# Graph network layer kernel: the first phase projects raw tiles with centred weights and finds each node's edge range by products on TensorE

## The chip, the cores and the metric

The kernel runs on one core of a Trainium2 chip. The metric is device time in microseconds (us) of one launch; smaller is better. Engines are TensorE (PE; PEld are its weight loads), VectorE (DVE), ScalarE (ACT), GpSimd (POOL) and SyncE (SP). A name with q (ACTq, SPq) is an engine's queue that issues a DMA.

## The reference

Two blocks of (graph layer, feed-forward layer) on 3125 nodes with 256 features and 50000 edges, sorted by target node. The change touches only what stands ahead of the first graph attention layer:

```python
def _layernorm(x, axis=-1, eps=1e-05):
    m = jnp.mean(x, axis=axis, keepdims=True)
    v = jnp.var(x, axis=axis, keepdims=True)
    return (x - m) / jnp.sqrt(v + eps)
...
        xh = (x @ W).reshape(N, H, D)
        a_src = jnp.einsum('nhd,hd->nh', xh, att_src)
        a_dst = jnp.einsum('nhd,hd->nh', xh, att_dst)
...
        e = jax.nn.leaky_relu(a_src[src] + a_dst[dst], NEG_SLOPE)
        m = jax.ops.segment_max(e, dst, num_segments=N)
...
    x = x + _L0_gnn_ref(_layernorm(x, axis=-1), edge_index, L0_gnn_W, ...)
```

The segment operations need, for each node, where its run of edges starts and ends in the sorted list.

## The kernel before

The program is a row of blocks; at the end of each all engines meet at a barrier, after their DMAs have landed. `first_phase` is the first block, `spread_phase` the second, `edge_phase` the third. Work inside a block is ordered by semaphores written out by hand; each engine runs its own list in order.

The nodes lie as NT = 25 tiles of P = 125 rows, in chunks of TB = 5 tiles. The edges lie as Q = 98 partitions with J = 4 pieces of EP = 128 edges each (`dstq`, `srcq`), and, turned by TensorE, as 128 partitions with ET = 392 columns (`dst_e`, `src_e`, `fwd_e`, `bwd_e`, `seat_e`).

`first_phase` does two things.

1. The projection. x is loaded whole into `res` (3 MB). After the whole has landed DVE takes each row's mean and variance (`norm_stats`), and ACT the root. Per chunk DVE writes the normed tiles `xn`, PE turns them (L359), ACT copies them out of the banks (L297), PE multiplies them with `w` (L366; 256 columns and 16 more for the attention sums, which DVE makes from W and att on L421 and L422), DVE adds the bias (L437). ACT's queue stores the result to the DRAM table `xh_tab`, SP's queue its last 8 columns to `adst_tab`.
2. The node bounds. For each node two counts: how many pieces of 128 edges begin ahead of it (15 tiles on DVE, L410, and 10 on ACT, L283, over the 392 first targets), then how many edges inside that piece lie ahead (L448). For the second count POOL gathers the piece of each node by 25 indirect DMAs (L331) from `dst_pad`, a copy of the targets in DRAM. The ends are the starts moved on by one node, which is done by a write to `start_tab` in DRAM and a read back (L260 to L263).

When `xh_tab` has landed POOL issues the 14 gathers of the first batch of edges (L176), still inside the block. `spread_phase` begins with 25 indirect scatters on POOL (L636), which need the bounds.

Of the kernel before, what the change touches and what calls it, by code (L numbers as in the profile page):

```python
# [19 lines left out]
I32 = mybir.dt.int32  # L20
U32 = mybir.dt.uint32
ALU = mybir.AluOpType
# [82 lines left out]
def setup(k):  # L105

    banks = k.ctx.enter_context(k.nc.psum_tensor("bank", [128, 8, 512], F32))
    k.ps = [banks[:, i, :] for i in range(8)]
# [23 lines left out]
    k.dst_pad = k.dram("dst_pad", [ET * EP])  # L132
    k.start_tab = k.dram("start_tab", [N + 1])
# [36 lines left out]
DVE_COUNTS = 15  # L170


# [7 lines left out]
def first_phase(k):  # L180
# [3 lines left out]
    ctx = ExitStack()  # L184
    with ctx:
        sb = lambda n, s, d=F32: k.sb(n, s, d, ctx)
        srcq_i, dstq_i = sb("srcq_i", [Q, J * EP], I32), sb("dstq_i", [Q, J * EP], I32)
# [3 lines left out]
        first_b = sb("first_b", [128, ET])  # L191
        last_b = sb("last_b", [128, ET])
        trash = sb("trash", [P, NT, ET])
        before = sb("before", [P, NT])
        tile = sb("tile", [P, NT])
        tiles_i = sb("tile_i", [128, NT], I32)
        tile_i = tiles_i[0:P, :]
        windows = sb("window", [128, NT, EP])
        window = windows[0:P, :, :]
        start, end, last = sb("start", [P, NT]), sb("end", [P, NT]), sb("last", [P, NT])  # L200
        has, t0 = sb("has", [P, NT]), sb("t0", [P, NT])
        total = sb("total", [1, 1])
        start_t, end_t = sb("start_t", [NT, P]), sb("end_t", [NT, P])
        starts_ready, starts_turned, ends_turned = k.sem("starts_ready"), k.sem("starts_turned"), k.sem("ends_turned")
# [4 lines left out]
        dummy = sb("no_edge", [1, RW])  # L209
        bias_in, bias_tail, dummies, dummies_out = k.sem("bias_in"), k.sem("bias_tail"), k.sem("dummies"), k.sem("dummies_out")  # L210
        xn = sb("xn", [P, TB, C])
        xt = sb("xt", [128, TB, 2, P])
        zeros = sb("zeros", [Q, J * EP // 2])
        zeroed, cleared, placed = k.sem("zeroed"), k.sem("cleared"), k.sem("placed")
        mark = sb("mark", [1, 1])
        w_in, att_in = k.sem("w_in"), k.sem("att_in")
        deviations, roots = k.sem("p_deviations"), k.sem("p_roots")
        w_ready = k.sem("w_ready")
        xn_made, xt_turned, xt_made = k.sem("p_xn_made"), k.sem("p_xt_turned"), k.sem("p_xt_made")
        projected, taken, out_done = k.sem("projected"), k.sem("p_taken"), k.sem("p_out_done")  # L220
        padded = k.sem("padded")
        edges_in = k.sem("edges_in")
        x_in = k.sem("x_in")
        banks_read = k.sem("banks_read")
        consts = k.sem("consts")
        edges_f = k.sem("edges_f")
        pad_out = k.sem("pad_out")
        turned = k.sem("turned")
        ends_b = k.sem("ends_b")
        tiles_found = k.sem("tiles_found")  # L230
        windows_in = k.gather_sem("windows_in")
        firsts_made, signs_summed, xh_done = k.sem("firsts_made"), k.sem("signs_summed"), k.sem("xh_done")
        half = sb("half", [P, NT])
        columns_made = k.sem("columns_made")
        starts_found = k.sem("starts_found")
        starts_out = k.sem("starts_out")
        ends_in = k.sem("ends_in")
        full = E // (J * EP)
        rest = E - full * J * EP
        even = full // 16 * 16  # L240

# [3 lines left out]
        def _(sp):  # L245
            sp.wait_ge(padded, 2)
            for a, t in ((k.a["dst"], dstq_i), (k.a["src"], srcq_i)):
                sp.dma_start(t[0:even, :], a[0:even * J * EP].rearrange("(q e) -> q e", e=J * EP)).then_inc(edges_in, 16)
            sp.wait_ge(edges_f, 1)
# [6 lines left out]
            for i in range(NT // TB):  # L256
                sp.wait_ge(taken, (i + 2) * TB)
                move(sp, adst_rows[:, i * TB:(i + 1) * TB, :], k.xh[:, i * TB:(i + 1) * TB, XW:RW], out_done)
# [12 lines left out]
        def _(act):  # L271
# [21 lines left out]
            for i in range(NT // TB):  # L293
# [4 lines left out]
                if i:  # L298
                    store(i - 1)
# [74 lines left out]
        def _(dve):  # L374
# [16 lines left out]
            for b, t in enumerate((k.dst_e, k.src_e, k.fwd_e, k.bwd_e, k.seat_e)):  # L391
# [3 lines left out]
                if b == 0:  # L395
                    dve.sem_inc(ends_b, 1)
# [2103 lines left out]
```

## Time and profile before

| | us |
|---|---|
| median of 3 runs | 1978.06 |
| lowest, highest | 1973.62, 1979.04 |
| the profiled execution, its time | 1977.53 |
| the profiled execution, its span | 1975.8 |

| engine | busy us of the span |
|---|---|
| PE | 1365.6 (69%) |
| PEld | 1134.1 (57%) |
| POOL | 1098.3 (56%) |
| DVE | 907.3 (46%) |
| ACT | 576.3 (29%) |

`first_phase` fills the first 100.6 us of the span. The profile gives every instruction's start and duration, the idle time of its engine just before it and what released it. A clock column shows what share of 2.4 GHz TensorE was granted: 1.00 is 2.4 GHz, 0.50 is 1.2 GHz.

### The profile page before, as it was taken

Reading aid. Unit: us, or ns where it says so; the run is one execution under the profiler, and the core shown is the slowest. Engines: PE = TensorE matmul, PEld = TensorE weight load, DVE = VectorE, ACT = ScalarE, POOL = GpSimd, SP = SyncE. Lnnn points to the kernel's source line nnn. Section 1 sums busy time; section 2 is a strip of 40 time slices with the busy share of each in tenths; the row PEclk is TensorE's granted clock in tenths of the full one; section 3 lists DMA queues with packets and bytes.
Section 4 is the critical chain, followed back from the end, with each engine's and each line's share of the span. In section 5 each row is a group of like instructions: output and inputs, shape, how many; then the busy total and the mean of one; then the engine's idle time right before and its main releaser. Section 6 shows DMA issues by size and latency. Waiting matters only on the chain. (4 is left out here: it accounts for less than half of the span.)

```text
span 1975.8 us, 23808 instructions
## 1 busy us (share of the span) xinstructions
PE 1365.6 (69%) x6688; PEld 1134.1 (57%) x6688; DVE 907.3 (46%) x1818; ACT 576.3 (29%) x1264; POOL 1098.3 (56%) x1086
## 2 busy tenths in 40 slices
PE   2435666656666266599999997656666666567998
PEld 2324544444454146599999997444445444346787
DVE  7425544444443667633333333644334333335953
ACT  2133433323333014133333332422222222222310
POOL 4477777777774600377222273077777777773520
PEclk7756878878878575699999999877878787978999
DMA  6484998888887601432111122743333333330002
GB/s 145 119 251 150 298 312 284 281 285 272 276 283 258 155 6 63 134 115 83 46 46 46 46 98 65 174 142 104 105 105 105 105 104 105 106 99 1 1 1 65
DMA packets 156809, 268.56 MB, mean 136 GB/s; under 512 B 26747, under 2 KB 119839, under 8 KB 155567
## 3 DMA queue, kind: packets, MB, share of 16 engines
q1 hardware_dynamic: 100252, 135.75, 22.1%
q0 software_dynamic: 46224, 123.97, 21.0%
q10 hardware_dynamic: 10213, 7.36, 1.5%
q8 instruction: 61, 1.00, 0.2%
q14 instruction: 59, 0.48, 0.1%
HBM read 169.82 MB, written 98.15 MB: 136 GB/s over the span
## 5 line engine op out<-in xcount | busy, mean ns | idle before, releaser
L1182 POOL DMA_INDIRECT sum_rows<-xn_tab,src_e x391 | 373.3, 955 | 174.5 <-issue 118.8
L1207 PE MATMUL bank<-sum_held,sum_hot 128*125 128x256 f32 x976 | 304.1, 474 | 195.3 <-ACT sum_held L1217 191.1
L798 POOL DMA_INDIRECT gat_rows<-xh_tab,src_e x363 | 343.4, 946 | 114.8 <-issue 107.8
L1207 PEld LDWEIGHTS bank<-sum_held,sum_hot 128*125 128x125 f32 x976 | 222.2, 236 | 273.5 <-issue 179.7
L871 PE MATMUL bank<-gat_rows,gat_same 128*128 128x264 f32 x784 | 263.7, 483 | 126.2 <-issue 126.2
L871 PEld LDWEIGHTS bank<-gat_rows,gat_same 128*128 128x128 f32 x784 | 176.6, 244 | 166.4 <-issue 132.6
L1217 ACT COPY sum_held<-sum_rows 128x1024 f32 x122 | 127.4, 1045 | 373.6 <-SPq L1173 334.1
L1894 PE MATMUL bank<-weights,e_xthigh 128*128 x896 | 220.3, 330 | 8.5 <-DVE e_xtlow L2049 5.4
L915 ACT COPY gat_outs<-bank 128x528 f32<-128x528 f32 x196 | 117.3, 598 | 281.8 <-PE bank L871 280.5
L2054 DVE TENSOR_TENSOR e_h<-e_gated,bank 128x342 f32<-128x342 f32 x112 | 57.1, 510 | 262.9 <-ACT e_gated L1987 262.9
L1239 DVE SCALAR_TENSOR_TENSOR res<-bank,prep_inv,res 125x256 f32 x122 | 58.9, 483 | 234.8 <-PE bank L1207 228.2
L1894 PEld LDWEIGHTS bank<-weights,e_xthigh 128*128 128x128 f32 x896 | 153.9, 192 | 17.9 <-issue 17.8
L1894 PE MATMUL bank<-weights,e_xtlow 128*128 x448 | 144.5, 323 | 0.0
L1915 PE MATMUL bank<-weights,e_hthigh 128*128 (+2 forms) x672 | 133.6, 294 | 0.3 <-DVE e_htlow L2059 0.3
L1987 ACT ACTIVATE e_gated<-bank 128x342 f32<-128x342 f32 x112 | 51.0, 455 | 239.2 <-PE bank L1894 239.2
L1773 POOL CAST weights<-staged 128x4264 fp32r<-128x4264 f32 x7 | 26.3, 3760 | 151.9 <-SPq L1832 142.8
L835 DVE TENSOR_TENSOR gat_rows<-gat_rows,bank 128x1792 f32<-128x1792 f32 x56 | 110.3, 2009 | 0.8 <-ACT bank L907 0.8
L1915 PEld LDWEIGHTS bank<-weights,e_hthigh 128*128 128x128 f32 (+2 forms) x672 | 102.5, 189 | 0.5 <-issue 0.5
L1915 PE MATMUL bank<-weights,e_htlow 128*128 x336 | 94.1, 280 | 0.0
L1894 PEld LDWEIGHTS bank<-weights,e_xtlow 128*128 128x128 f32 x448 | 85.9, 192 | 0.0
L819 DVE TENSOR_TENSOR gat_logit<-gat_rows,adst_e 128x112 f32<-128x112 f32 x28 | 7.8, 277 | 165.8 <-DMA gat_rows<-xh_tab,src_e 165.8
L1225 DVE TENSOR_TENSOR sum_hot<-bank,walk_local 128x2000 f32<-128x2000 f32 x31 | 69.0, 2225 | 2.2 <-DMA prep_bias<-in_L_gnn_b_dram 2.2
(508 smaller groups left out, 2416.8 us busy)
## 6 DMA issues: line engine op xcount, KB each, us to landing
parts<-gat_outs SPq DMA_DIRECT2D x27, 1904.0 KB, 8.0
staged<-w_tab SPq DMA_DIRECT2D x8, 2132.0 KB, 8.9
w_tab<-w_stage SPq DMA_DIRECT2D x16, 682.0 KB, 10.6
w_raw<-in_L_ffn_w_dram SPq DMA_DIRECT2D x16, 640.0 KB
gat_rows<-xh_tab,src_e POOLq DMA_INDIRECT x391, 4.7
sum_rows<-xn_tab,src_e POOLq DMA_INDIRECT x391, 2.8
w_tab<-w_stage SPq DMA_DIRECT2D x8, 768.0 KB, 10.6
weights<-y_tab SPq DMA_DIRECT2D x10, 600.0 KB
```

Of the source, the lines that this page charges most:

```text
L798: pool.indirect_dma_start(out=rows[b % R][:, t, :], out_offset=None, in_=k.xh_tab, in_offset=bass.IndirectOffsetOnAxis(ap=k.src_e[:, b * S ...
L835: v.tensor_tensor(f, f, weight[b % 2][:, t0 * H:t1 * H].rearrange("p (t h a) -> p t h a", h=H, a=1).to_broadcast([EP, SB // 2, H, D]), ALU ...
L871: m = nc.tensor.matmul(k.pairs[duo % DUOS][:, t % 2, 0:sums_w], same[b % 2][:, t, :], rows[b % R][:, t, 0:sums_w], start=True, stop=True)
L915: nc.scalar.copy(outs[b % 2][:, t:t + 2, 0:sums_w], k.pairs[duo % DUOS][:, :, 0:sums_w]).then_inc(taken, 1)
L1182: pool.indirect_dma_start(out=rows[:, at // IP % (RING * GPAIRS), at % IP, :], out_offset=None, in_=k.xn_tab, in_offset=bass.IndirectOffse ...
L1207: m = nc.tensor.matmul(k.ps[s][0:P, 0:C], hot[g % 2][:, s, c, :], held[:, s, c, :], start=(c == 0), stop=(c == IP - 1))
L1217: nc.scalar.copy(held_pair(n), pair).then_inc(staged, 1)
L1225: v.tensor_tensor(hot[g % 2][:, :, :, :], lane.rearrange("p (a b n) -> p a b n", a=1, b=1).to_broadcast([EP, IB, IP, P]), w.local[:, g * I ...
L1239: v.scalar_tensor_tensor(out=into, in0=k.ps[s][0:P, 0:C], scalar=prep.inv[:, bass.ds(node, 1)], in1=into, op0=ALU.mult, op1=ALU.add).then_ ...
L1894: last = nc.tensor.matmul(bank[:, 0:HH[a]], xt[s][px][:, c, :], part(slot, up_at(m, pw, c) + HB[a], 128, HH[a]), start=(n == 0), stop=(n = ...
L1915: m = nc.tensor.matmul(DOWN[s][:, 0:C], ht[a][ph][0:rows, b, :], part(slot, down_at(pw, 3 * a + b), rows, C), start=(a == 0 and n == 0), s ...
L2054: v.tensor_tensor(h[a][:, 0:HH[a]], gated[a][:, 0:HH[a]], GATE[a][:, 0:HH[a]], ALU.mult).then_inc(h_made, 1)
```

## The change

The x load is split into five chunk loads that start right behind the edge loads. The raw tile is turned and multiplied; the mean is taken out by centring the weights instead (each column of `w` less its mean, which PE sums with a matrix of ones and DVE subtracts), and 1/deviation is multiplied in when DVE takes the product. Statistics are made per chunk. The transposes of one tile stand ahead of the product of the tile before.

The bounds need no gathers. `passed[q, j, n]` is 1 where node n is beyond the first edge of piece j of partition q: four comparisons on POOL, each 98x3125. `rises` holds the differences between each piece of 128 targets and the piece before. The product of `passed` and `rises`, summed over all pieces (four matmuls per tile), is the piece that a node's run begins in; column 128 counts the pieces. The second count is then made from the bank, three tiles of each chunk on DVE and two on ACT. The ends come from two small products of `start` with a shifted identity and a corner matrix. The joins table is made for 8 partitions, later, in `spread_phase`. `dst_pad`, `start_tab`, the window gathers and the piece counts over 392 columns are gone.

```diff
         @block.sync
         def _(sp):
-            sp.wait_ge(padded, 2)
+            sp.wait_ge(padded, 3)
             for a, t in ((k.a["dst"], dstq_i), (k.a["src"], srcq_i)):
                 sp.dma_start(t[0:even, :], a[0:even * J * EP].rearrange("(q e) -> q e", e=J * EP)).then_inc(edges_in, 16)
-            sp.wait_ge(edges_f, 1)
-            sp.dma_start(k.dst_pad.rearrange("(q e) -> q e", q=Q), dstq[:, :]).then_inc(pad_out, 16)
-            move(sp, k.res[:, :, :], k.a["x"].rearrange("(t p) c -> p t c", p=P), x_in)
+            for c in range(CHUNKS):
+                move(sp, k.res[:, c * TB:(c + 1) * TB, :], x_rows[:, c * TB:(c + 1) * TB, :], x_in[c])
             sp.wait_ge(zeroed, 1)
...
+            for c in range(CHUNKS):
+                tiles = slice(c * TB, (c + 1) * TB)
+                sp.wait_ge(taken, (c + 1) * TB)
+                move(sp, xh_rows[:, tiles, :], k.xh[:, tiles, 0:XW], xh_done)
+            for c in range(CHUNKS):
+                tiles = slice(c * TB, (c + 1) * TB)
+                move(sp, adst_rows[:, tiles, :], k.xh[:, tiles, XW:RW], adst_out)
...
         @block.gpsimd
...
+            me(pool, nc.gpsimd.iota(node_row, pattern=[[1, N]], base=0, channel_multiplier=0, allow_small_or_imprecise_dtypes=True))
+            pool.wait_ge(firsts_made, 1)
+            for j in range(J):
+                nc.gpsimd.tensor_scalar(passed[:, j, :], node_row, first_dst[:, j:j + 1], None, ALU.is_gt).then_inc(passed_made, 1)
...
-            for t in range(NT):
-                pool.indirect_dma_start(out=windows[:, t, :], out_offset=None, in_=k.dst_pad.rearrange("(a b) -> a b", b=EP),
-                                        in_offset=bass.IndirectOffsetOnAxis(ap=tiles_i[:, t:t + 1], axis=0)).then_inc(windows_in, 16)
             pool.wait_ge(columns_made, 1)
-            pool.wait_ge(xh_done, 32 * (NT // TB))
+            pool.wait_ge(xh_done, 32 * CHUNKS)
             gather_batch(k, pool, 0)
...
         @block.tensor
...
+            pe.wait_ge(passed_made, J)
+            pe.wait_ge(rises_made, 1)
+            pe.wait_ge(taken, NT)
+            for t in range(NT):
+                c, s = t // TB, t % TB
+                if c:
+                    pe.wait_ge(tiles_kept, c)
+                    if s < BY_DVE:
+                        pe.wait_ge(counted, (c - 1) * BY_DVE + s + 1)
+                    else:
+                        pe.wait_ge(signed, (c - 1) * (TB - BY_DVE) + s - BY_DVE + 1)
+                for j in range(J):
+                    last_mm = nc.tensor.matmul(k.ps[XR + t % XP][0:P, 0:WIN], passed[:, j, t * P:(t + 1) * P], rises[:, j, :], start=(j == 0), stop=(j == J - 1))
+                last_mm.then_inc(windows, 1)
...
         @block.vector
...
+            for c in range(CHUNKS):
+                if c < CHUNKS - 1:
+                    spreads(c + 1)
+                take(c)
+            me(dve, v.tensor_copy(rises[:, 0, 0:EP], prev_i[:, :]))
...
+                dve.wait_ge(signed, (c + 1) * (TB - BY_DVE))
+                v.tensor_copy(tile[:, c * TB:(c + 1) * TB], k.banks[0:P, XR:8, EP]).then_inc(tiles_kept, 1)
```

The next excerpts are the engines' own lists. POOL, before, from the attention mask table to the first gathers (`window` is the piece gathered for each node of a tile):

```order
L324 AFFINE_SELECT sel<-sel 8x256
L326 AFFINE_SELECT sel<-sel 8x256
L331 DMA window<-dst_pad,tile_i 128x128 x25
L176 DMA gat_rows<-xh_tab,src_e 128x264 x14
L185 UNCONDITIONAL_BRANCH
```

POOL, of the change, from the row of lane numbers (`minus`) on:

```order
L288 IOTA minus 98x512
L289 MEMSET p_bias 125x16
L290 IOTA passed 98x3125
L293 TENSOR_SCALAR passed<-passed,first_dst 98x3125 x4
L294 MEMSET zeros 98x256
```

The 25 gathers are gone, and one long iota and four long comparisons stand where POOL had short setup work; the 14 gathers still end its list in the block. DVE, before, from the edges' landing to the first column table:

```order
L379 CAST dstq<-dstq_i 98x512
L381 CAST srcq<-srcq_i 98x512
L383 TENSOR_TENSOR same<-dstq 98x511
L384 MEMSET same 98x5
L385 COPY cont_q<-same 98x512
L386 TENSOR_SCALAR tile_dst<-dstq 98x4
L388 SCALAR_TENSOR_TENSOR seat<-same,minus 98x512
L389 SCALAR_TENSOR_TENSOR seat<-same,seat 98x512
L390 TENSOR_SCALAR same<-same 98x513
L393 COPY dst_e<-bank 128x4x98
```

DVE, of the change, the last of the same steps and what follows:

```order
L385 SCALAR_TENSOR_TENSOR seat<-same,seat 98x512
L386 TENSOR_SCALAR same<-same 98x513
L390 TENSOR_TENSOR prod<-w,att 128x512
L391 TENSOR_REDUCE w<-prod 128x2x8
L390 TENSOR_TENSOR prod<-w,att 128x512
L391 TENSOR_REDUCE w<-prod 128x2x8
L395 COPY dst_e<-bank 128x4x98
L395 CAST src_e<-bank 128x4x98
L395 COPY fwd_e<-bank 128x4x98
L395 COPY bwd_e<-bank 128x4x98
L395 COPY seat_e<-bank 128x4x98
L400 SCALAR_TENSOR_TENSOR w<-bank,w 128x272 x2
```

The nine edge steps keep their order; the work on the weights moves ahead of the five column copies, and the centring follows them. PE, of the change, the last tile of the second count's products and the block's end; nothing like it was there before, when L369 and L371 turned `start` and its shifted copy:

```order
L358 MATMUL bank<-rises,passed 125x129 [waits signed,tiles_kept]
L358 MATMUL bank<-rises,passed 125x129 x3
L362 MATMUL bank<-start,ident 125x25 [waits starts_made,corner_made]
L363 MATMUL bank<-start,corner 125x25
L183 UNCONDITIONAL_BRANCH
```

## Rows read from the trace of the kernel before

**Rows 1.** Timeline, the block's last 27 us: start, duration, engine, line [idle <-releaser].

```profile
73.39 0.36 ACTq L141 DMA_DIRECT2D xh_tab<-xh  x1
...
79.67 0.94 POOL L176 DMA_INDIRECT gat_rows<-xh_tab,src_e  x1 [21.29 <-DMA xh_tab<-xh]
...
85.42 0.18 DVE L455 COPY end<-bank 125x25 f32<-125x25 f32 x1 [4.39 <-PE bank L371]
...
87.33 0.18 DVE L466 TENSOR_SCALAR start_row<-t 125x25 int32<-125x25 f32 x1
...
95.92 0.94 POOL L176 DMA_INDIRECT gat_rows<-xh_tab,src_e  x1 [0.30 <-issue]
...
100.73 0.23 DVE L685 MEMSET tails<- 125x200 f32 x1 [13.22 <-PEq L185]
```

**Rows 2.** Timeline, the first instruction of the third block.

```profile
163.43 0.29 DVE L804 COPY bank<-lane 128x128 f32<-128x128 f32 x1 [7.28 <-PEq L604]
```

**Rows 3.** Timeline, DVE and POOL while both work on the first tables.

```profile
5.21 0.48 DVE L379 CAST dstq<-dstq_i 98x512 f32<-98x512 int32 x1 [4.06 <-DMA srcq_i<-in_src_dram]
5.48 0.46 POOL L324 TENSOR_SCALAR_AFFINE_SELECT sel<-sel 8x256 f32<-8x256 f32 x1
...
5.72 0.49 DVE L381 CAST srcq<-srcq_i 98x512 f32<-98x512 int32 x1
6.00 0.47 POOL L326 TENSOR_SCALAR_AFFINE_SELECT sel<-sel 8x256 f32<-8x256 f32 x1
...
6.14 0.88 DVE L383 TENSOR_TENSOR same<-dstq 98x511 f32<-98x511 f32 x1
```

**Rows 4.** Groups of POOL instructions: count | busy us, mean ns | idle before.

```profile
L1774 POOL TENSOR_TENSOR weights<-staged,weights 128x4264 fp32r<-128x4264 f32 x7 | 65.6, 9372 | 0.6
...
L1773 POOL CAST weights<-staged 128x4264 fp32r<-128x4264 f32 x7 | 26.3, 3760 | 151.9 <-SPq L1832 142.8 <-DMA staged<-w_tab 9.1
...
L1188 POOL CAST att_w_high<-att_w_comb 128x1024 fp32r<-128x1024 f32 x1 | 1.1, 1055 | 0.0
...
L308 POOL IOTA minus<- 98x512 f32 x1 | 0.6, 577 | 0.1
```

**Rows 5.** DMA issues in the first 102 us: count, size, us from issue to landing.

```profile
att<-in_L_gnn_att_dst_dram ACTq DMA_DIRECT2D x1, 128.0 KB, 9.7
```

**Rows 6.** Timeline: edge steps of DVE, a column copy, a product on the weights.

```profile
7.60 0.68 DVE L388 SCALAR_TENSOR_TENSOR seat<-same,minus 98x512 f32<-98x512 f32 x1
...
9.65 0.43 DVE L390 TENSOR_SCALAR same<-same 98x513 f32<-98x513 f32 x1
...
11.08 0.87 DVE L393 COPY dst_e<-bank 128x392 f32<-128x392 f32 x1 [1.01 <-PE bank L344]
...
26.66 0.69 DVE L421 TENSOR_TENSOR prod<-w,att 128x512 f32<-128x512 f32 x1
```

**Rows 7.** Timeline, DVE's row statistics; PE in the second chunk of the projection.

```profile
30.77 8.27 DVE L473 BATCH_NORM_STATS2 stats<-res 125x6 f32<-125x256 f32 x25 [1.25 <-DMA res<-in_x_dram]
...
48.62 1.60 PE L359 MATMUL bank<-ident,xn 125*128 125x125 f32 x10
...
54.65 0.59 PE L359 MATMUL bank<-ident,xn 125*128 125x125 f32 x4
```

**Rows 8.** Busy time by stretch: us, PE, PEld, DVE, ACT, POOL, PEclk, DMA, GB/s.

```profile
41.40:44.50 3.10, 3.06 (x13) 2.69 (x14) 2.81 (x9) 1.83 (x5) 2.49 (x3) 0.50 0.22 63
...
72.90:75.60 2.70, 0.00 (x0) 0.00 (x0) 2.68 (x18) 0.00 (x0) 0.00 (x0) 0.93 0.47 91
```

**Rows 9.** Timeline, first and last of twelve products of 128 columns on PE.

```profile
1910.39 0.39 PE L2265 MATMUL bank<-t_token,att_square 128*128 128x128 f32 x2
...
1912.84 0.39 PE L2267 MATMUL bank<-att_square,t_token 128*128 128x128 f32 x2
```

**Rows 10.** Timeline, one of ACT's signed counts over 392 columns.

```profile
17.10 0.60 ACT L283 ACTIVATE trash<-first_b,half 125x392 f32<-125x392 f32 x1
```

**Rows 11.** Groups of PE instructions: the products of 98 rows and 124 columns.

```profile
L994 PE MATMUL bank<-walk_pick,dstq 98*128 98x124 f32 x8 | 2.1, 440 | 0.0
```

More of the change, by code:

```diff
@@ L190, in first_phase @@
         seat, seat0, minus = sb("seat", [Q, J * EP]), sb("seat0", [Q, J * EP]), sb("minus", [Q, J * EP])
[L191 to L200, printed above, removed]
+        first_dst, rises = sb("first_dst", [Q, J]), sb("rises", [Q, J, WIN])
+        passed = sb("passed", [Q, J, N])
+        node_row = passed[:, J - 1, :]
+        trash = sb("trash", [P, TB, EP])
+        before, tile = sb("before", [P, NT]), sb("tile", [P, NT])
+        start, last, corner = sb("start", [P, NT + 1]), sb("last", [P, NT]), sb("corner", [P, P])
         has, t0 = sb("has", [P, NT]), sb("t0", [P, NT])
-        total = sb("total", [1, 1])
-        start_t, end_t = sb("start_t", [NT, P]), sb("end_t", [NT, P])
-        starts_ready, starts_turned, ends_turned = k.sem("starts_ready"), k.sem("starts_turned"), k.sem("ends_turned")
+        half = sb("half", [P, NT])
         w = sb("w", [128, 2, RW])
@@ L302, in _ @@
+            act.wait_ge(halves_made, 1)
+            for c in range(CHUNKS):
+                for t in range(c * TB + BY_DVE, (c + 1) * TB):
+                    act.wait_ge(windows, t + 1)
+                    nc.scalar.activation(trash[:, t % TB, :], k.ps[XR + t % XP][0:P, 0:EP], ACT.Sign, bias=half[:, t:t + 1], scale=-1.0,
+                                         accum_out=before[:, t:t + 1]).then_inc(signed, 1)
         @block.gpsimd
@@ new lines, in take @@
+            def take(c):
+                rstd = k.rstd[:, c * TB:(c + 1) * TB]
+                dve.wait_ge(roots, c + 1)
+                me(dve, v.reciprocal(rstd, rstd))
+                for t in range(c * TB, (c + 1) * TB):
+                    dve.wait_ge(projected, t + 1)
+                    v.scalar_tensor_tensor(out=k.xh[:, t, :], in0=k.ps[XR + t % XP][0:P, 0:RW], scalar=k.rstd[:, t:t + 1], in1=bias[:, :], op0=ALU.mult, op1=ALU.add).then_inc(taken, 1)
+            spreads(0)
+            dve.wait_ge(prev_in, 16)
@@ new lines, in _ @@
+            signs = before[:, :].rearrange("p (c s) -> p c s", s=TB)[:, :, BY_DVE:TB]
+            dve.wait_ge(tiles_kept, CHUNKS)
+            dve.wait_ge(counted, CHUNKS * BY_DVE)
+            me(dve, v.tensor_scalar(signs, signs, 0.5, 0.5 * EP, ALU.mult, ALU.add))
+            v.scalar_tensor_tensor(out=start[:, 0:NT], in0=tile[:, :], scalar=float(EP), in1=before[:, :], op0=ALU.mult, op1=ALU.add).then_inc(starts_made, 1)
+            dve.wait_ge(starts_made, 1)
+            me(dve, v.tensor_scalar(t0[:, :], start[:, 0:NT], -float(NO_ROW + 1), None, ALU.add))
```

273 lines of the change are left out of this document (117 added, 156 removed).

## The prediction

> **What bounds the kernel now.** I read the timeline of the first block from its end backwards, since a block ends for all engines together. [rows 1] show the end. DVE is done with the bounds at 87.5 us. POOL starts its 14 gathers at 79.67, when the last piece of `xh_tab` has landed, 6.3 us after its store was issued at 73.39, and issues the last at 95.92. The next block starts at 100.6 (DVE's first instruction there at 100.73), 3.7 us behind POOL's last. So two chains matter: projection, landing, gathers (it ends last), and projection, window counts, bounds (13 us shorter). The second block needs the bounds at once and runs, as far as I can see, unchanged: it ends at 163.4 [rows 2], paced by POOL's own list. Three DVE steps that it gains (the joins table, about 1.1 us) stand where DVE later waits for a DMA. So I take each us by which the first block ends earlier as one us of the whole, and the question is where that end goes.
>
> **Step 1: when the weights are ready.** The projection now starts when the centred weights are there, and these stand behind DVE's edge steps. There the change puts long POOL work beside them. [rows 3] show what that does. DVE's second cast ends at 6.21, 0.27 behind POOL's end at 5.94; POOL's next ends at 6.47, 0.26 behind that; DVE's comparison ends at 7.02, 0.55 behind that. Each ends one bare pass over its data after the other's end: the two engines take turns, they don't overlap. The Trainium skill, page "SBUF — State Buffer", section "Who interferes with whom", states this as a lock held for a whole instruction between GpSimd and a DVE instruction in a two-port mode or with two SBUF inputs; the trace agrees, by the 0.27 us above, and it speaks against this change.
>
> What a comparison of 98x3125 costs on POOL no row shows. With one input the nearest are the casts: 3.760 us for 4264 columns and 1.055 for 1024 [rows 4], so 0.835 ns a column: 2.65 us. With two inputs it is 9.37 for 4264, so 2.2 ns: 6.9 us. I take 2.65, since the comparison reads one tile. (The page "GPSIMD Engine Reference", section 3.1, of the Trainium skill gives 1.03 cycles an element at 1.2 GHz for a body of one or two operations: 2.7 us by estimate, which no run here shows yet, and would leave the sum as it is.)
>
> The iota of 3125, by L308's 577 ns for 512 columns [rows 4], costs 2.7 to 3.5, say 3.0; it starts at about 3.4 behind short setup (an estimate from instructions like those in the same place), so POOL is free at 6.4. The edges are in at 5.2 as before. Then in turns: DVE's cast 0.27, comparison, cast 0.27, comparison, DVE's equality 0.55, comparison, copy 0.27, comparison. That is 6.4 + 1.35 + 4 x 2.65 = 18.35. Behind it DVE still has from L388 to L390, 7.60 to 10.08 [rows 6], 2.5 us: 20.85. Four products and sums on the weights at 0.72 from start to start (L421, 0.69 long) are 2.9: 23.75; att has landed by then, as it took 9.7 us from its issue in the crowd of x [rows 5] and now is issued about 2 us earlier. Five column copies at 0.89 [rows 6] are 4.45: 28.2. Two centrings of 272 columns, like the bias sums, 0.45 each, and a little hand-over: the weights are ready at about **29.4**. x has its chunk loads in by then.
>
> **Step 2: the projection.** Before, a chunk took 54.65 - 48.62 = 6.03 us on PE [rows 7]. The same matmuls run now, in another order, the copy of a tile hidden behind the product of the tile before. DVE per chunk has five statistics (8.27 / 25 = 0.33 each), small steps of about 1.1 us and five products, 5 us in all, under PE's 6.03. So 25 tiles are 30.1. At the start the clock is at 0.50 for 3.1 us [rows 8], which loses 1.5, and 0.7 is the filling. PE ends at 29.4 + 32.3 = 61.7, the last tile is taken at 62.4.
>
> **Step 3: POOL's chain.** 6.3 for the landing, 17.2 from first gather to the end of the last, 3.7 to the next block [rows 1]: 89.6. The `adst_tab` stores now stand behind the `xh_tab` stores in SP's queue and don't delay them.
>
> **Step 4: the bounds.** DVE makes `rises` in five steps behind its last tile, an estimate of 1.2 us: 63.6. Then 25 tiles of four products with 129 columns. Twelve products of 128 columns take 1912.84 + 0.22 - 1910.39 = 2.67 us at clock 1.00 [rows 9], 0.223 each, so 0.90 a tile and **22.5** in all. PE cannot run into the next chunk before all five counts of the last one are made and the piece numbers copied: PE's own tail 0.2, ACT's count (0.60 at 392 columns [rows 10], less 264 columns at about 0.9 ns, and its read-out, so 0.5), DVE's copy and hand-overs 0.3, together 1.0, five times 5.0. Ends: 91.1. Then two small DVE steps 0.4, the two products 0.7, and seven steps on 125x25; the ten from L455 to L466 took 2.1 [rows 1], so 1.5, and 0.5 for the barrier. That is **94.2**, 4.6 later than POOL's chain: the bounds become what ends the block.
>
> The pause before PE's products is 2 us. Before, PE stopped at 72.9 and its clock still stood at 1.00 for most of the next 2.7 us, 0.93 on average [rows 8]. Should it drop to 1.2 GHz, it comes back as at the start, for 1.7 us.
>
> **Sum.** 100.6 - 94.2 = 6.4 us earlier. Terms removed outright (25 window gathers, the counts over 392 columns, L448, the DRAM round trip of 4.4 us) lay off the chain that ended last, or are in the new chain's place already. Against the profiled execution's 1977.5 that gives 1971.1; the median of the runs, 1978.06, is 0.5 higher, and gives 1971.6. I forecast **1971.4**, a gain of 0.33% on the median. A gain of 0.3%, about what a measurement of this kernel can tell from no change, is 5.9 us, so the forecast sits just beyond it. The unknown terms (iota 0.4, comparison up to 0.3 each, hand-overs) make it 1968 to 1976 by itself.
>
> **Rivals.**
> - *DVE is not held up.* If DVE's steps get in first each time, the edges are done by 11, the weights wait for att (issued at about 3.9, an estimate, and 9.7 to land [rows 5]: 13.6), and are ready at 13.6 + 2.9 + 4.5 + 1.0 = 22.0. The whole gain is 7.4 more: 1964. For it: POOL must wait for `first_dst` and needs a hand-over; against it: in [rows 3] POOL got its turn each time. Chance 0.15.
> - *The comparisons are slow.* At the two-input price of 6.9 they cost 17 more, the block ends at 111 and the kernel takes 1988: **slower**. It decides from 2.65 + 6.4 / 4 = 4.25 us each, 1.35 ns a column, on. For it: no comparison with a column operand is in the trace; against it: one input. Chance of over 4.25 us: 0.13, a third of it between 4.2 and 5.7, which would still be within 0.3%.
> - *PE stays at 1.2 GHz in step 4.* There a record of 98x124 comes each 0.26 us (2.1 / 8, [rows 11]), so 2.1 a tile: 30 us more, 2001. Against it: PE is busy 4.5 of 5.5 us there. Chance 0.04.
> - *The gathers still end the block*, so that the bounds don't count. It needs the landing to take over 4.6 us longer than before; the time would be 1972 to 1976. Chance 0.08.
>
> **How the numbers follow.** The forecast's own case has 0.60. It splits about 0.32 beyond 0.3% and 0.28 within. Faster: 0.32 + 0.15 + 0.02 = 0.49. Within 0.3%: 0.28 + 0.05 + 0.06 = 0.39 (some comparisons of middling price, the gathers' case). Slower: 0.12. The range goes from 1963, which takes in the free DVE, to 1979; beyond it lie slow comparisons and the slow clock, about 0.15.
>
> **What would show it.** The timeline of the first block: four comparisons of 2.65 us on POOL with one DVE instruction between each, and DVE's casts lengthened to nearly 3 us; the first transposes at 29 to 30; 6 us a chunk; `xh_tab` gathers from 68; products on `passed` at 0.9 us a tile with five gaps of 1 us; the next block at 94. It is wrong if the comparisons are much longer, if DVE's edge steps keep their old times, if PE's chunks take over 6.5, or if the gap at a chunk's end is over 2 us.

## The result: slower, by the comparisons on POOL

The changed kernel takes 1990.84 us (median of 5 runs, 1986.72 to 1991.58) against 1977.89 for the kernel before in the same comparison (1973.62 to 1979.04): the ratio is 1.0071, 95% interval 1.0057 to 1.0084. Forecast were 1971.4, with 1963 to 1979 around it. The direction was wrong, and the time lies beyond the range; it is near where the rival of the slow comparisons put it (1988). The profiled execution took 1991.58, its span is 1989.7.

The profile page of the changed kernel shows where to look. Each digit is a slice of 50 us, in tenths:

```profile
PE   1953666666657356399999998656666666557998
...
DVE  8534544344444477733333333644333343435953
...
POOL 8166777777775600277222274077777777773520
```

In the first slice TensorE does next to nothing, while DVE and POOL both read 8. DVE's timeline there (start, duration, line) says what the 8 is made of:

```profile
6.22 0.42 DVE L375 CAST dstq<-dstq_i 98x512 f32<-98x512 int32 x1
...
6.68 8.33 DVE L377 CAST srcq<-srcq_i 98x512 f32<-98x512 int32 x1
14.93 0.67 DVE L379 TENSOR_TENSOR same<-dstq 98x511 f32<-98x511 f32 x1
...
15.77 8.09 DVE L381 COPY cont_q<-same 98x512 f32<-98x512 f32 x1
...
23.85 6.75 DVE L384 SCALAR_TENSOR_TENSOR seat<-same,minus 98x512 f32<-98x512 f32 x1
30.63 1.23 DVE L385 TENSOR_TENSOR_SCAN seat<-same,seat 98x512 f32<-98x512 f32 x1
31.96 9.18 DVE L386 TENSOR_SCALAR same<-same 98x513 f32<-98x513 f32 x1
41.06 0.67 DVE L390 TENSOR_TENSOR prod<-w,att 128x512 f32<-128x512 f32 x1
```

Two casts of the same shape stand in the first two rows, one of 0.42 us and one of 8.33. An instruction's duration counts the time in which it waits for its turn, so the second did its 0.4 us of work at the end of 8. Four steps are stretched like this. In [rows 6], in the kernel before, the step that is L384 here took 0.68 (L388 there) and the one that is L386 here 0.43 (L390 there). What they wait for is the group of the four comparisons on POOL (duration in ns, least, median, most):

```profile
L293 POOL TENSOR_SCALAR passed<-passed,first_dst x4: 8183/8288/8852, 6.5 to 31.9; 98x3125 f32<-98x3125 f32 x4
```

8.2 to 8.3 us each, where the forecast took 2.65: 2.6 ns a column instead of 0.85. The longest, 8.85, is the second one: it starts at 14.73, just as DVE's L379 gets its 0.67 us, and is itself the one that waits. The fourth comparison starts at 31.90 and ends at 40.08. DVE's L386 ends only at 41.14: behind the comparisons it waited through some of POOL's short instructions as well.

The rest of the block, from the weights to the next block, in one timeline:

```profile
49.68 1.10 PE L334 MATMUL bank<-ident,res 125*128 125x125 f32 x4 [3.02 <-DVE w L400]
...
80.90 0.50 DVE L420 SCALAR_TENSOR_TENSOR xh<-bank,rstd,p_bias 125x272 f32<-125x272 f32 x1 [0.42 <-PE bank L344]
...
81.43 0.32 SPq L139 DMA_DIRECT2D xh_tab<-xh  x1
...
82.80 4.67 PE L358 MATMUL bank<-rises,passed 98*125 98x129 f32 x40 [1.94 <-DVE rises L434]
...
87.02 1.18 POOL L171 DMA_INDIRECT gat_rows<-xh_tab,src_e  x1 [43.35 <-DMA xh_tab<-xh]
...
88.21 4.70 PE L358 MATMUL bank<-rises,passed 98*125 98x129 f32 x40 [0.75 <-DVE tile L442]
...
103.50 0.95 POOL L171 DMA_INDIRECT gat_rows<-xh_tab,src_e  x1 [0.30 <-issue]
...
109.76 0.17 DVE L442 COPY tile<-bank 125x5 f32<-125x5 f32 x1 [1.90 <-ACT trash L273]
...
113.17 0.23 DVE L679 MEMSET tails<- 125x200 f32 x1 [0.61 <-PEq L183]
```

The last row answers to the last of [rows 1], which stood at 100.73: the next block opens 12.44 us later. DVE's idle time before it was 13.22 us and is 0.61: before, DVE had long been done and POOL's gathers ended the block; now the bounds end it, as forecast, only that the whole chain starts 20 us too late.

**The account, step by step.**

| | forecast | measured |
|---|---|---|
| edge steps done | 20.85 | 41.06 |
| from there to the weights ready | 8.55 | 8.56 (49.62) |
| weights ready to the last tile taken | 33.0 | 31.8 (81.40) |
| last tile taken to the next block | 31.8 | 31.8 (113.17) |
| next block opens | 94.2 | 113.17 |

The first row carries the error; the others are right within 1.2 us.

The block accounts for 12.4 of the 13.9 us between the two spans (1989.7 - 1975.8). 1.2 more lie in the second block: the third opens at 177.09, 63.92 us behind 113.17, and by [rows 2] it took 62.70 before. The three joins steps of DVE are not it, for the load of `sparse` in that block is issued 37.1 us after the block's start and 36.8 before; its landing takes the rest. The same distance is 62.4 to 65.2 us in the nine other profiles below of kernels with the changed prologue's code, and 61.9 and 62.6 in the two made from the kernel before, so about 1 us probably belongs to the change. Its cause stays open.

### The profile page after: what moved, and what is told of

Its sections match the earlier page's. It is cut to its first block and busy times, and to the rows that moved or that the text cites. A ratio compares the mean times of both kernels' runs of the same rounds, so it can differ in the third digit from the quotient of the medians.

```text
span 1989.7 us, 24160 instructions
## 1 busy us (share of the span) xinstructions
PE 1389.8 (70%) x6890; PEld 1157.9 (58%) x6890; DVE 925.2 (47%) x1768; ACT 576.6 (29%) x1268; POOL 1111.6 (56%) x1068
## 5 line engine op out<-in xcount | busy, mean ns | idle before, releaser
L1913 PE MATMUL bank<-weights,e_htlow 128*128 x336 | 94.2, 280 | 0.0
L1857 POOL DMA_INDIRECT y_tab<-e_x,slot_row x52 | 50.9, 979 | 34.1 <-ACT e_x L1995 20.4
## 6 DMA issues: line engine op xcount, KB each, us to landing
w_tab<-w_stage SPq DMA_DIRECT2D x16, 682.0 KB, 10.6
w_tab<-w_stage SPq DMA_DIRECT2D x8, 768.0 KB, 10.6
```

Source lines behind the costliest of these rows:

```text
L1913: m = nc.tensor.matmul(DOWN[s][:, 0:C], ht[a][ph][0:rows, b, :], part(slot, down_at(pw, 3 * a + b), rows, C), start=(a == 0 and n == 0), s ...
```

## Experiments

The theory after the result has two parts. **Price:** a tensor-scalar instruction costs 2.6 ns a column on POOL, whatever it computes. **Turns:** DVE's steps that read and write SBUF in certain forms can't run beside it, so that its length goes into the chain. Rivals: only the comparison, or the column operand, is that slow; the hold is from reading alone; or not the hold but the 33 us of POOL time sets the end.

The measure in each is the time at which the next block opens. The rest of the kernel, profiled time less that, was 1873 to 1884 us in all the profiles, so one profile tells the whole time only to some 5 us, but the block's own end within about 1. Runs of different groups were timed on different chips, so they are compared by their ratios to the kernel before. Four of the runs have one timing each; their times are set beside the kernel before of their own group. Code in this part is shortened to the lines that matter.

### Other forms in POOL's idle time

Four instructions are added to the changed kernel, at a place where POOL waits anyway; nobody reads what they write.

```diff
+ nc.gpsimd.tensor_scalar(probe, node_row, 1000.0, None, ALU.is_gt)
+ nc.gpsimd.tensor_scalar(probe, node_row, first_dst[:, 1:2], None, ALU.subtract)
+ nc.gpsimd.tensor_copy(probe, node_row)
+ nc.gpsimd.tensor_scalar(probe[:, 0:1560], node_row[:, 0:1560], first_dst[:, 1:2], None, ALU.is_gt)
```

> Four probes are added on POOL behind its setup, where it waits for the table: a comparison with a constant instead of a column operand, a subtraction with the column operand, a plain copy, and the comparison at half width (1560 columns). They write a spare tile, so nothing is left out. Theory A (the price lies in POOL's comparison itself): constant 8.2 us, half width 4.2 us, subtraction and copy about 2.7 us, as the casts' 0.835 ns a column. Theory B (every scalar operation on POOL costs this, whatever the operation): constant, subtraction 8.2, copy 2.7. Theory C (turns with DVE made the comparisons long, their own price is 2.65): constant and column forms here near 2.7 to 3.5, half width 1.4, since DVE's work beside them is short. The time is of no interest, but DVE's small steps with two SBUF inputs stand beside the probes: if these wait for the probes the projection ends some 10 to 20 us later.

Time 1998.64 us, a single one, against a median of 1982.15 for before in its group. Timeline of POOL and DVE:

```profile
43.79 8.12 POOL L310 TENSOR_SCALAR gat_rows<-passed 98x3125 f32<-98x3125 f32 x1
...
52.01 8.21 POOL L311 TENSOR_SCALAR gat_rows<-passed,first_dst 98x3125 f32<-98x3125 f32 x1
53.78 4.60 DVE L414 TENSOR_TENSOR spread<-stats 125x5 f32<-125x5 f32 x1
...
60.29 2.79 POOL L312 COPY gat_rows<-passed 98x3125 f32<-98x3125 f32 x1
...
63.18 4.22 POOL L313 TENSOR_SCALAR gat_rows<-passed,first_dst 98x1560 f32<-98x1560 f32 x1
...
63.41 3.09 DVE L417 TENSOR_TENSOR spread<-spread,gap 125x5 f32<-125x5 f32 x1
```

A constant instead of the column operand 8.12, a subtraction instead of a comparison 8.21, half the columns 4.22: all 2.6 to 2.7 ns a column. The plain copy is 2.79, 0.89 a column, the price that the forecast took from [rows 4]. So the casts there were right as casts and said nothing of a scalar operation. The page "GPSIMD Engine Reference", section 3.1, of the Trainium skill prices a body of one or two operations at 1.03 cycles an element, 2.7 us here by estimate; the runs speak against that for tensor-scalar (8.2 us) and for it with the copy (2.79), and the measurement decides.

So the second of the three theories holds: the price is that of a scalar operation, not of the comparison, and the turns with DVE did not make it. The probes cost nothing by themselves, since POOL waits there, and yet the first gather comes at 90.26, 3.2 later than in the changed kernel: DVE's 0.17 us steps on 125x5, caught in turns, took 4.60 and 3.09, and the projection waits for them. The next block opens at 118.06, 4.9 later; the rest lies in the bounds' first products, which took 6.32 us in the first chunk and not 4.67.

### The same load in the kernel before

An iota and two comparisons are added to the kernel before, ahead of its window gathers, which POOL reaches only at 26.9.

```diff
+ flat = windows[0:Q, :, :].rearrange("p t e -> p (t e)")[:, 0:N]
+ nc.gpsimd.iota(flat, pattern=[[1, N]], base=0, channel_multiplier=0)
+ for _ in range(2):
+     nc.gpsimd.tensor_scalar(flat, flat, k.node[0:Q, 1:2], None, ALU.is_gt)
```

> The kernel before, with one iota of 3125 columns and two comparisons of 98x3125 added on POOL behind its setup, at 6.5 us, where it has nothing to do until 26.9; they end at about 26. Nothing is left out. Theory A (DVE is shut out for the length of each): DVE's steps from its equality on take 10 to 17 us longer in sum, the first block ends at 110 to 117 instead of 100.6, the time is 1988 to 1994. Rival (long comparisons harm only what waits for their results): DVE keeps its times, the block ends at 100.6 and the time is 1978.

Time 1987.75 us, a single one, 5.6 above the median of before in its group (1982.15, 1978.04 to 1983.50). The next block opens at 110.56 instead of 100.73: 9.8 later, for 19.5 us of work on an engine that has nothing to do at that time.

```profile
7.27 2.27 DVE L389 COPY cont_q<-same 98x512 f32<-98x512 f32 x1
9.36 16.80 POOL L331 TENSOR_SCALAR window<-window,node 98x3125 f32<-98x3125 f32 x2
...
9.53 6.78 DVE L392 SCALAR_TENSOR_TENSOR seat<-same,minus 98x512 f32<-98x512 f32 x1
16.34 1.23 DVE L393 TENSOR_TENSOR_SCAN seat<-same,seat 98x512 f32<-98x512 f32 x1
17.67 0.43 DVE L394 TENSOR_SCALAR same<-same 98x513 f32<-98x513 f32 x1
...
19.11 0.87 DVE L397 COPY dst_e<-bank 128x392 f32<-128x392 f32 x1 [1.01 <-PE bank L348]
```

This shows the cost with everything else of the change left out. It also shows what is not held: the copies that read PSUM (0.87, as in [rows 6]) run inside the second comparison, 17.72 to 26.16. The first comparison ends at 17.62; the step of 6.78 us got in ahead of that end, and the scan ran right behind it in the same stretch, so whether a scan would be held earlier in a comparison is not shown. That is why two comparisons and an iota cost 9.8 and not 19.5.

### Instructions that only write

Seven iotas of the same size instead, 19.8 us in sum.

```diff
+ for _ in range(7):
+     nc.gpsimd.iota(flat, pattern=[[1, N]], base=0, channel_multiplier=0)
```

> The kernel before with seven iotas of 98x3125 added on POOL at the start, 7 x 2.74 = 19.2 us, whose output nobody reads: about as long as the iota and two comparisons that cost the kernel before some 9.5 us (gathers from 36.8 instead of 26.9) in an earlier run. An iota only writes. Theory (POOL holds DVE's two-input and fast one-input steps for whole instructions, whatever POOL executes): DVE steps at 6 to 25 take 2.7 us instead of 0.4 to 0.9, each held to the end of the iota that runs, and the first gather moves from 26.9 to about 29 to 36. Rival (only instructions that read are in the way): DVE's steps keep their 0.4 to 0.9 us, and the gathers start at about 27 to 28, once POOL is through with its own 19.2 us (29 at the latest).

```profile
6.43 19.83 POOL L330 IOTA window<- 98x3125 f32 x7
...
7.18 2.27 DVE L388 COPY cont_q<-same 98x512 f32<-98x512 f32 x1
9.38 2.74 DVE L389 TENSOR_SCALAR tile_dst<-dstq 98x4 int32<-98x4 f32 x1
9.44 2.68 DVE L391 SCALAR_TENSOR_TENSOR seat<-same,minus 98x512 f32<-98x512 f32 x1
...
23.79 0.57 DVE L410 TENSOR_TENSOR joins<-last_b 128x391 f32<-128x391 f32 x1
```

A copy or a scalar step from SBUF to SBUF is held by an instruction that only writes: the copy takes 2.27, and a scalar step of 98x4 elements takes 2.74, as long as the iota. So for these the rival of reading alone is out. For steps with two SBUF inputs it holds. L410, with both inputs in SBUF, runs at 23.79 inside the last iota (23.52 to 26.26) and takes 0.57, and 0.56 in the kernel before. L391 has 2.68 only because it stands behind the held L389: both end at 12.12, when the second iota has just ended (the third starts at 12.16), so its own 0.68 us of work was done while that iota ran. The comparisons, which read SBUF, hold such a step; the iota does not. The window gathers start at 34.10 (26.92 before) and the next block at 106.19, 5.5 later. The single time, 1979.66, is 3 above its group's median of before and doesn't resolve that.

### Comparisons held back until the weights are ready

```diff
  pool.wait_ge(firsts_made, 1)
+ pool.wait_ge(w_ready, 1)
  for j in range(J):
```

> The changed kernel, its four comparisons on POOL held back until the weights are ready; nothing else differs. Theory (the comparisons cost time only where DVE's steps must wait for them, and their own length has cover elsewhere): the weights are ready at about 22 (13.5 + 4 x 0.72 + 4.45 + 0.9), not at 49.6; the comparisons then run from 22 to 56 beside the projection, and DVE's steps that take turns with POOL are held there: the projection, 32 us in the clear, is stretched by up to 20 us. Between them the time lies anywhere from 1966 to 1985, below the changed kernel's 1991. Rival (not the turns, but the 33 us of comparisons themselves set the end, through the products that read them): the comparisons end at 56 and the rises at 57 in any case, so 1966 to 1968. Rival 2 (a hold costs the same wherever it falls): 1991.

Time 1975.36 us, a single one, against a median of 1976.39 for before in its group (1971.60 to 1979.81), which does not tell them apart. The weights are ready at 21.4, and the comparisons run from 21.66 to 54.4 beside the projection:

```profile
21.66 8.21 POOL L294 TENSOR_SCALAR passed<-passed,first_dst 98x3125 f32<-98x3125 f32 x1 [15.51 <-DVE w L401]
```
```profile
23.11 4.92 DVE L410 TENSOR_TENSOR spread<-stats 125x5 f32<-125x5 f32 x1
...
30.29 5.94 DVE L410 TENSOR_TENSOR spread<-stats 125x5 f32<-125x5 f32 x1
36.84 2.14 DVE L421 SCALAR_TENSOR_TENSOR xh<-bank,rstd,p_bias 125x272 f32<-125x272 f32 x5
38.89 1.72 DVE L408 BATCH_NORM_STATS2 stats<-res 125x6 f32<-125x256 f32 x5
40.65 3.75 DVE L410 TENSOR_TENSOR spread<-stats 125x5 f32<-125x5 f32 x1
```

The same four comparisons, moved by one wait, give back 15.9 us (next block at 97.28). One small step in each chunk is held, 18.4 us in four; the projection ends about 11 us later than in the run with signs on ACT below. The rival by which the comparisons' own end matters is out: they end at 54.4, the last take (DVE's step that brings a tile's product out of the bank) at 65.5. Row statistics keep their 1.72 for five inside a comparison, and the takes, with one operand in PSUM, their 2.14 for five across the start of the third one (38.05).

### The comparisons on DVE, and on ACT

First on DVE, behind its edge steps:

```diff
-     nc.gpsimd.tensor_scalar(passed[:, j, :], node_row, first_dst[:, j:j + 1], None, ALU.is_gt)
+     nc.vector.tensor_scalar(passed[:, j, :], node_row, first_dst[:, j:j + 1], None, ALU.is_gt)
```

> The changed kernel with the four comparisons moved from POOL to DVE, behind its edge steps; POOL only makes the row of node numbers. Theory A (the whole loss is POOL's comparisons and the turns DVE takes with them): a comparison on DVE costs 1.7 us (3125 columns at two a cycle of 0.96 GHz, like the cast of 512 in 0.27 us), the four 6.9; edge steps done at 11.5, weights ready at about 28, the block ends at 28 + 63.4 = 91.5, the time is 1968 to 1971, ratio to before 0.995 to 0.9965. Rival (the rest of the change loses too, and would without the comparisons): the block ends after 100, 1978 or more.

1972.21 us, ratio 0.9948 (0.993 to 0.9965). Then on ACT as signs, with the scales of what reads them adapted:

```diff
-     nc.gpsimd.tensor_scalar(passed[:, j, :], node_row, first_dst[:, j:j + 1], None, ALU.is_gt)
+     nc.scalar.activation(passed[:, j, :], node_row, ACT.Sign, bias=first_dst[:, j:j + 1], scale=1.0)
...
- v.tensor_copy(tile[:, c * TB:(c + 1) * TB], k.banks[0:P, XR:8, EP])
+ v.tensor_scalar(tile[:, c * TB:(c + 1) * TB], k.banks[0:P, XR:8, EP], 0.5, 0.5 * (J * Q - 1), ALU.mult, ALU.add)
```

> The changed kernel with the comparisons made on ACT as signs (+1 or -1 in place of 1 or 0); DVE compares with twice the node number less 3125 and halves the piece counts, so the result is the same. Theory A: four signs of 98x3125 at about 0.9 ns a column are 11 to 12 us on ACT, which has nothing else to do until the projection, and DVE keeps its old times; edge steps done at 11.5, weights wait for att at 13 to 14 and are ready at 21 to 22.5, the block ends at 84.5 to 86, the time is 1961 to 1964, ratio 0.992 to 0.993. Rival (something else than the port holds the weights, such as att or x in the crowd of loads): weights ready at 28 or later, time above 1969.

1964.94 us, ratio 0.9917 (0.9894 to 0.994); timed again on another chip, 1965.55, ratio 0.9927 (0.9911 to 0.9944).

> The changed kernel with the comparisons as signs on ACT once more, as a measure for the two others on this chip: ratio to before 0.992 as in its first timing.

The rows of the two, DVE's and ACT's:

```profile
11.07 7.25 DVE L388 TENSOR_SCALAR passed<-passed,first_dst 98x3125 f32<-98x3125 f32 x4
...
59.31 6.32 PE L357 MATMUL bank<-rises,passed 98*125 98x129 f32 x40 [1.94 <-DVE rises L436]
```
```profile
12.01 11.27 ACT L263 ACTIVATE passed<-passed,first_dst 98x3125 f32<-98x3125 f32 x4
```

A comparison takes 1.81 us on DVE, 2.82 on ACT and 8.2 on POOL. On ACT it hides wholly: DVE's edge steps are done at 12.2, with their old durations, and the weights are ready at 21.94 (the case of the rival "DVE is not held up": 22.0, measured 21.94; its time of 1964 is a ratio of 0.993 to before, measured 0.9917 and 0.9927). The next block opens at 85.92, 27.2 us earlier than in the changed kernel, and the weights are ready 27.7 us earlier. With the comparisons on DVE the weights come at 26.57 and the next block at 91.34; of those 5.4 us 4.6 are the later weights. The first chunk of products lost 1.65, 6.32 us in place of 4.67, at a granted clock of 0.50 (1.2 GHz) from 61 to 64, and the projection was 0.9 shorter.

So the chunkwise projection and the bounds on TensorE are a gain of 0.7 to 0.8%, and their comparisons on POOL turn it into a loss of 0.7%.

### What ends the block: without the chunk gates, and without the pause

The forecast had the bounds end the block 4.6 us behind the gathers. To see both chains, the run with signs on ACT is shortened in two steps. First TensorE waits for the copy of one tile's piece number in place of a chunk's:

```diff
  if c:
-     pe.wait_ge(tiles_kept, c)
+     pe.wait_ge(tiles_kept, t - TB + 1)
```

> The kernel with the comparisons as signs on ACT, and besides: each tile's piece number is copied by DVE on its own (25 copies of 0.17 us), and TensorE waits for the copy of the tile whose bank it takes, not for a whole chunk's. Theory (the bounds' chain ends the block, with a gap of about 1.0 us ahead of each chunk of products, and the gathers' chain ends 4.6 to 5 us earlier): the gaps at the four later chunks and the wait after the last one shrink to nothing, the products run 25 x 0.89 = 22.3 us in one piece from 56.0, so that the bounds end near 81.5 and the gathers' chain (last gather 76.25 + 4.7 = 81) takes over as the end: the block ends near 81.5 instead of 85.9, and the time falls by 4 to 5 us, from 1964.9 to about 1960.5. Rival 1 (something else opens the next block): no change, 1964.9. Rival 2 (the extra copies hold up DVE's counts, 0.35 + 0.17 and their fixed parts a tile, and the gap comes back in small pieces): a fall of 1 to 2 us, 1963.5.

1960.24 us, ratio 0.9914 (0.9895 to 0.9933). The profiled execution was the slowest of its five, 1969.00. In it the next block opened at 84.67, only 1.25 earlier. The windows of TensorE (length, then busy time and count of PE, PEld, DVE, ACT and POOL, then granted clock) say why:

```profile
56.00:58.00 2.00, 1.73 (x9) 1.76 (x10) 0.31 (x4) 0.00 (x0) 0.00 (x0) 0.61 0.89 208
58.00:60.00 2.00, 2.00 (x12) 2.00 (x12) 0.54 (x5) 0.00 (x0) 0.00 (x0) 0.53 0.69 123
60.00:62.00 2.00, 2.00 (x21) 2.00 (x20) 0.75 (x6) 0.20 (x1) 1.22 (x2) 1.00 0.35 21
```

The gaps are gone, but the clock fell to its lower level (0.5 is 1.2 GHz) for most of 4 us behind the pause of 1.94, and 12 matmuls a window stand where 21 could. The 200 matmuls took 24.04 us. The same kernel again:

> The run without the chunk gates once more, on the same chip as the one after it, since the two were timed on different chips: by the traces (next block at 84.67 against 85.92 us) it should be 1.2 us below the run with the comparisons as signs on ACT, at a ratio to before of about 0.991. If the granted clock keeps its level in the first products, 2.6 us more.

1960.60 us, ratio 0.9914 (0.9899 to 0.9929). This time the clock stayed at 1.00, the 200 matmuls took 22.38 us, 1.66 less, and the next block opened at 81.83, 2.96 before the signs run of the same chip (84.79). Then the pause itself is taken out, with the rises made in DVE's idle time ahead of the last chunk's takes:

```diff
- pe.wait_ge(taken, NT)
  for t in range(NT):
+     if t < XP:
+         pe.wait_ge(taken, NT - XP + t + 1)
```

> The run without the chunk gates, and besides DVE computes the rises ahead of the last chunk's takes (in its idle time there), and TensorE's first five products wait each for the take of their own bank, not for all 25 takes. In the run without the gates TensorE stood idle for 1.94 us between the last projection product (54.34) and the first product of the bounds (56.27), the granted clock was 0.61 and 0.53 in the two windows after it (56 to 60), and the 25 products took 24.8 us instead of 22.2. Theory (the pause costs its 1.94 us and the clock behind it 2.6 us; the gathers' chain stands 2.4 us behind the bounds' and takes over): the bounds' part would end 4.5 us earlier, near 79.5, but the last gather starts at 76.94 and the next block 4.8 us later, at 81.7, so the next block opens at 82 to 82.5 instead of 84.67: 2.4 us less than the run without the gates, that is a ratio of about 0.990 to before. Rival 1 (the clock falls all the same, from another pause): 1.9 us less at most, next block at 82.8. Rival 2 (DVE's rises hold up the takes of the last chunk and with them the store and the gathers): no gain or a loss of 1 us.

1957.46 us, ratio 0.9896 (0.988 to 0.9912). Medians of the three on this chip: 1965.55, 1960.60, 1957.46. The intervals of the ratios overlap from one to the next, so the steps rest on the traces more than on the times.

```profile
53.03 22.30 PE L362 MATMUL bank<-rises,passed 98*125 98x129 f32 x200
...
77.17 0.95 POOL L171 DMA_INDIRECT gat_rows<-xh_tab,src_e  x1 [0.30 <-issue]
...
79.11 0.18 DVE L471 TENSOR_SCALAR main_row<-last 125x25 int32<-125x25 f32 x1
80.94 0.23 DVE L690 MEMSET tails<- 125x200 f32 x1 [1.65 <-PEq L183]
```

Here the end changes hands: DVE is done at 79.29 and waits 1.65 us, where it waited 0.6 in the runs that the bounds ended. The last gather starts at 77.17 and lands 2.8 us later, at about 80.0, behind DVE's end, so the gathers most likely end this block. From the start of the last gather to the next block are 3.8 us; in [rows 1] it was 4.8 (95.92 to 100.73). The forecast's 3.7, counted from the last gather's end, is thus 2.8 here, and why is open. The next block opens at 80.94, 0.9 earlier than in the run with the full clock. The 2.4 that had been expected were counted from the profile with the low clock (84.67), against which it is 3.7. The first gather came at 60.70, 6.9 us after its store, where it had taken 5.6 in the run before it. Why it landed later isn't settled; the takes were not held up (store at 53.76, and 53.72 there).

### The weights centred ahead of the column copies

Built on the run without chunk gates. DVE centres the weights first, and two of ACT's comparisons go in pieces between its copies of the projection.

```diff
+ dve.wait_ge(w_summed, 1)
+ for c in range(2):
+     m = v.scalar_tensor_tensor(out=w[:, c, :], in0=k.ps[0][:, 0:RW], scalar=-1.0 / C, in1=w[:, c, :], op0=ALU.mult, op1=ALU.add)
+ m.then_inc(w_ready, 1)
  for b, t in enumerate((k.dst_e, k.src_e, k.fwd_e, k.bwd_e, k.seat_e)):
...
- dve.wait_ge(w_summed, 1)
- for c in range(2):
-     m = v.scalar_tensor_tensor(out=w[:, c, :], in0=k.ps[0][:, 0:RW], scalar=-1.0 / C, in1=w[:, c, :], op0=ALU.mult, op1=ALU.add)
- m.then_inc(w_ready, 1)
```

> As the run without the chunk gates, and besides DVE centres the weights ahead of the five column copies (4.45 us), and of the four comparisons on ACT two run in 12 pieces of 521 columns between the copies of the projection, so that ACT is free when the weights are. Theory (weights ready starts the whole chain, everything behind it is rigid): the weights are ready at 17.5 instead of 21.95, and the block's end moves with them, by up to 4.4 us; the first projection waits for the column copies until 22 while transposes run ahead of it, so 3 us is the middle: end of block near 78.5, time about 1957.5 (3 below the run without the gates). Rival (ACT or DVE becomes the bound in the projection: ACT at 0.60 + 0.33 us a tile plus its fixed parts against the 1.13 us a tile of the chunks, or DVE's spreads and takes that start after the copies anyway): no gain, within 1 us of the run without the gates, about 1960.5.

1964.93 us, ratio 0.9943 (0.9923 to 0.9962): no gain. The weights were ready 2.7 us earlier, at 18.6, but the first product of the projection came at 23.11, and at 23.27 without it: its bank holds a column table until DVE's copies end, at 22.90 here. The outcome is the rival's, no gain, but by the column copies and not by ACT or DVE inside the projection. That the median is 4.7 us above the run without chunk gates, while the next block opens at 84.53 in both within 0.2, is not explained.

## Why the prediction was wrong

- **What bounds the kernel, and that the two chains are projection, landing, gathers and projection, bounds:** right. The block's shift is found again in the span, 12.4 of 13.9.
- **Step 1, the price of a comparison: the step that failed.** "With one input the nearest are the casts ... So 0.835 ns a column: 2.65 us." Measured 8.2 to 8.3. The term was chosen by the number of inputs; the runs show that the kind of operation sets it: copy 2.79, comparison or subtraction 8.12 to 8.21. The two-input price of 6.9, the other one worked out, was too low as well. The four together took 33.6 us and not 10.6, 23.0 more. The edge steps came 20.2 later. The forecast had counted DVE's turns (1.35) and the steps behind the comparisons (2.5) on top, and all but the last of them fell inside the longer comparisons; that last step waited 1.0 beyond their end.
- **Step 1, the turns:** right in kind, and what makes the price cost time. The comparisons ended at 40.08, far ahead of the products that need them (from 63.6 in the forecast), so by these times they would have been hidden without the turns; the held-back run shows 15.9 us given back with the price unchanged. Which DVE steps take turns was too simple: all edge steps up to the copy were counted as waiting for a whole comparison, while two-input steps get in before its end, and copies out of PSUM and row statistics run on. The section "Who interferes with whom" of the page "SBUF — State Buffer" in the Trainium skill names DVE steps in two-port modes, and those with two SBUF inputs beside a GpSimd instruction that reads SBUF. The trace agrees with both kinds: casts and copies took 8.1 to 8.3 and a two-input step 6.75 beside the comparisons, and a two-input step kept its 0.57 beside an iota.
- **Iota 3.0, edges in at 5.2, the 8.55 to the weights:** 2.74, 5.97, 8.56.
- **Step 2:** 33.0 against 31.8. A chunk takes 5.67 us (store to store, 75.97 to 81.43 is the last 5.5), not 6.03. The slow start was there: four products took 2.18 us at 50.81 and 1.08 later on.
- **Step 3:** landing 5.6 (6.3), gathers to the end of the last 17.4 (17.2). By this chain the block would have ended at 108.2, 5.0 ahead of the bounds; forecast were 4.6. The 3.7 behind the last gather's end is the forecast's own term; where the gathers did end the block, it was 2.8.
- **Step 4:** 0.89 a tile (0.90), 5.44 a chunk with its gap (5.5), from the last take to the next block 31.8 (31.8). The 1.7 us named for a drop of the clock is right too, where it came: 1.65.
- **The rivals.** The slow comparisons were the right one, at 0.13. Its place and its sign hold, and its price was 1.4 short of the measured one. That its 1988 lies so near the measured 1990.84 is in part luck: by its own sum 8.25 us a comparison gives 1994. Its threshold of 4.25 us is not tested. Since the nearest rows spread from 0.84 to 2.2 ns a column and no row had the form itself, 0.60 for the case at the low end was too much. "DVE is not held up" gives the time that the signs on ACT reach. "PE stays at 1.2 GHz" came for three to four us in four of the profiles, never for the whole step.

## What to carry to other kernels

Price an instruction on POOL by a row of its own kind: a scalar operation there costs three times a copy of the same tile, and more than four times the same operation on DVE. Before work goes to POOL because POOL is idle, look at what DVE does at that time: each plain cast, copy or scalar step from SBUF to SBUF may be held as long as the POOL instruction lasts, however small it is, and each DVE step with two SBUF inputs for some three quarters of a scalar operation on POOL. ACT held nobody up, and the comparisons had cover there in full.

## What the runs showed of the hardware

- **A two-input step gets in before a tensor-scalar on POOL ends, always at the same part of it.** In the held-back run comparisons start at 21.66 and 29.88, and the held steps of 0.17 us end at 28.03 and 36.23, so they start 6.2 us into the comparison. In the probes it is 6.2 us (58.38 less 0.17, from 52.01) for the whole width and 3.15 (66.50 less 0.17, from 63.18) for half of it; in the kernel before with two comparisons added 6.27 (16.31 less 0.68, from 9.36). So they get in after some three quarters of a tensor-scalar on POOL; casts and copies wait to its end. An iota did not hold a two-input step at all (0.57 inside it) but held one-input steps to its end. Both would fit if a two-input step waited only for POOL's reading; no run shows when that ends.
- **POOL's tensor-scalar goes by columns alone:** 2.60 ns (8.12 / 3125) to 2.71 (4.22 / 1560), for comparison and subtraction, constant and column operand.
- **The same pause of 1.94 us** ahead of the bounds' products was followed by the full granted clock in the changed kernel and in four more profiles, and by the lower level in four others, where it cost 1.65 us each time (6.32 against 4.67 for 40 matmuls, 24.04 against 22.38 for 200). The two profiles of the kernel without chunk gates have it once each way. No rule of it was found; without the pause it didn't happen in the one profile taken.
- **The clock column can read 1.00 where matmuls run at half pace:** in the changed kernel four products take 2.18 us at 50.81 and 1.08 later, with 1.00 in both stretches. The pace of the first stretch is read here from the durations.
